# 23 more products of constants on TensorE in the head of a quantized Hadamard FFN

## What is computed

```python
def reference(x, itok, L0_cond_weights, w_up, w_down):
    w = L0_cond_weights[itok]                        # (64, 64, 64)
    h = einsum('bct,bcd->bdt', x, w)                 # projection
    h = hbitlinear(h, w_up, 8)                       # 512 -> 1024
    h = jnp.square(jax.nn.relu(h))
    return x + hbitlinear(h, w_down, 8)              # 1024 -> 512

def hbitlinear(x, w, bits):
    xq = act_quant(fwht(x), bits)      # Hadamard along the last axis, absmax rounding per token
    wq = weight_quant(w)               # round(w / mean|w|), clipped to -1..1, times mean|w|
    return einsum('bsd,fd->bsf', xq, wq)
```

## Time and profile before

| | us |
|---|---|
| median of 3 timed runs | 263.11 |
| lowest and highest of them | 262.69, 263.40 |
| the profiled execution | 261.73 |
| its span, first to last instruction | 259.7 |
| TensorE busy | 247.4 (95%) |
| VectorE busy | 207.1 (80%) |
| ScalarE busy | 147.5 (57%) |
| GpSimd busy | 107.9 (42%) |

### The profile page before, as it was taken

How to read it: one execution, slowest core, us unless ns; L and a number is a source line. 1 busy time by engine, 2 the same in 40 slices (tenths; PEclk the granted TensorE clock), 3 DMA queues, 4 the chain that set the end, 5 groups by cost and what they waited for, 6 DMA issues and landing times. The chain is left out here.

```text
span 259.7 us, 6271 instructions
## 1 busy us (share of the span) xinstructions
PE 247.4 (95%) x2172; PEld 205.7 (79%) x2172; DVE 207.1 (80%) x344; ACT 147.5 (57%) x210; POOL 107.9 (42%) x135
## 2 busy tenths in 40 slices
PE   8589999998999999999999999999999999989994
PEld 8478898987898788878897787978898887757651
DVE  0548679988788697989878986989898888999482
ACT  0378887676554775475656365565775646651330
POOL 1000006661624508080806444372936445786710
PEclk9959999999999999999999999999999999999999
DMA  3995061475268444675564881464535657424523
GB/s 106 361 373 180 16 213 32 59 180 98 52 161 130 87 163 82 122 174 118 141 91 121 189 198 36 79 203 85 130 71 126 167 139 107 121 79 121 128 105 138
DMA packets 63441, 34.29 MB, mean 132 GB/s; under 512 B 53554, under 2 KB 53682, under 8 KB 63410
## 3 DMA queue, kind: packets, MB, share of 16 engines
q10 hardware_dynamic: 48370, 12.95, 28.3%
q1 hardware_dynamic: 15040, 20.95, 25.3%
HBM read 13.70 MB, written 8.39 MB: 85 GB/s over the span
## 5 line engine op out<-in xcount | busy, mean ns | idle before, releaser
L373 POOL TENSOR_TENSOR p<-g 128x512 f32<-128x512 f32 x64 | 80.8, 1286 | 128.1 <-DVE g L1237 128.1
L907 PE MATMUL h_ps<-zqT,w_upT 128*128 128x256 f16 x512 | 63.5, 273 | 0.7 <-DMA zqT<-zq 0.7
L930 PE MATMUL u_ps<-had_sb,p 128*128 128x128 f32 x480 | 58.8, 276 | 1.2 <-ACT uq L566 1.2
L930 PEld LDWEIGHTS u_ps<-had_sb,p 128*128 128x128 f32 x480 | 56.7, 192 | 3.5 <-ACT uq L566 1.7
L962 PE MATMUL o_ps<-w_downT,uqT 128*128 128x512 f16 x240 | 56.7, 379 | 0.2 <-DVE uqT L1211 0.2
L907 PEld LDWEIGHTS h_ps<-zqT,w_upT 128*128 128x128 f16 x512 | 49.3, 98 | 8.7 <-issue 0.9
L526 ACT ACTIVATE g<-h_ps 128x512 f32<-128x512 f32 x64 | 37.3, 595 | 26.9 <-PE h_ps L907 19.3
L566 ACT ACTIVATE uq<-u_ps,u_mul 128x1024 f16<-128x1024 f32 x30 | 33.4, 1113 | 33.0 <-DVE u_mul L1255 29.1
L1244 DVE TENSOR_REDUCE u_max<-u_ps 128x1 f32<-128x1024 f32 x30 | 36.6, 1220 | 11.3 <-PE u_ps L930 10.9
L962 PEld LDWEIGHTS o_ps<-w_downT,uqT 128*128 128x128 f16 x240 | 23.4, 98 | 22.3 <-issue 0.4
L1232 DVE TENSOR_TENSOR g<-g 128x1024 f32<-128x1024 f32 x32 | 40.8, 1300 | 0.1
(11 more groups left out here) (52 smaller groups left out, 126.4 us busy)
## 6 DMA issues: line engine op xcount, KB each, us to landing
xs<-in_x_dram SPq DMA_DIRECT2D x16, 512.0 KB, 3.8
out_dram<-out_sb SPq DMA_DIRECT2D x32, 256.0 KB, 2.3
w_raw<-in_L_ffn_w_down_dram SPq DMA_DIRECT2D x4, 512.0 KB, 5.9
w_raw<-in_L_ffn_w_up_dram ACTq DMA_DIRECT2D x2, 512.0 KB, 6.0
w_raw<-in_L_ffn_w_up_dram SPq DMA_DIRECT2D x2, 512.0 KB, 6.8
ws<-in_L_cond_weights_dram SPq DMA_DIRECT2D x62, 16.0 KB, 2.6
uqT<-uq ACTq DMA_TRANSPOSE x30, 3.5
zqT<-zq ACTq DMA_TRANSPOSE x15, 4.0
```

What stands on the lines that cost most here:

```text
L373: nc.gpsimd.tensor_tensor(new[:, :, m, :], old[:, :, 0, :], old[:, :, 1, :], (ALU.add, ALU.subtract)[m]).then_inc(s_p8[k], 1)
L907: mm = nc.tensor.matmul(h_ps[:, u % 2, i, :].rearrange("p (k n) -> p k n", k=KP), w_upT[:, q, f * P:(f + 1) * P], zqT[t % NZT][:, :, q, :] ...
L930: mm = nc.tensor.matmul(home[:, c * P:(c + 1) * P], p8[t % 2][:, c, k * P:(k + 1) * P], had_sb[:, :], start=True, stop=True)
```

## The change

The loop of `warm` becomes a helper, `idle(n, home)`, which issues n products of `ones` with itself into a given place. `warm` has 17 of them instead of 16, now into the first 128 columns of h_ps. 4 more stand before project(0), 10 before had_z(0, 1), 6 before weight_sum(0) and 2 before first_turn(0); these write columns 256 to 383 of o_ps, which nobody reads before `down` writes them. That makes 39 products instead of 16. The helper has no wait of its own and signals nothing. The lists of ScalarE, VectorE, GpSimd and SyncE are as they were.

```diff
-WARM = 16
+WARM = 17
...
             def warm():
                 pe.wait_ge(s_const, 1)
-                for i in range(WARM):
-                    nc.tensor.matmul(o_ps[:, 0:P], ones[:, :], ones[:, :], start=True, stop=True)
+                idle(WARM, h_flat[:, 0:P])
+
+            def idle(n, home):
+
+                for i in range(n):
+                    nc.tensor.matmul(home, ones[:, :], ones[:, :], start=True, stop=True)
...
             warm()
+            idle(4, o_ps[:, 2 * P:3 * P])
             project(0)
+            idle(10, o_ps[:, 2 * P:3 * P])
             had_z(0, 1)
+            idle(6, o_ps[:, 2 * P:3 * P])
             weight_sum(0)
             had_z(0, 0)
             project(1)
             weight_turn(0, 1)
             weight_turn(0, 0)
+            idle(2, o_ps[:, 2 * P:3 * P])
             first_turn(0)
             first_turn(1)
             had_z(1, 0)
```

## The result

The changed kernel takes 259.8 us in the median (259.37 to 260.16), the kernel before 262.9 us (262.45 to 263.40) beside it. The ratio is 0.9881, with a 95% interval from 0.9855 to 0.9907: 3.1 us faster, 1.2%. The prediction said 261.4 us and a range from 260.2 to 263.2.

What follows compares the result with a forecast made beforehand. TensorE was taken to bound the kernel after the head. Savings of 0.2, 0.92 and 0.59 us sum to 1.7; the 1.73 us inherited through VectorE, off 263.11, gives 261.4 us, range 260.2 to 263.2.

Steps and rivals of the forecast that it cites:

- The bound: TensorE has nothing left to give after the head, so a microsecond won in the head should reach the end.
- The price of a product, and the four places: 0.22 us each at full clock, 0.44 at half; at most 0.1 us late before project(0), had_z(0,1), weight_sum(0) and first turn.
- The clock: In the head, filling TensorE's waits removes the 6.82 us stretch at 0.50 (12.40 to 19.22); granted clock stays 1.00.
- The sum for the profiled execution: weight_sum(0) 0.2, had_z(0,0) 0.92, project(1) 0.59 us; VectorE's y_outer(1,1) passes on 1.73 us, up(0,1) at 22.43, span 258.0.
- From the profile to the time: Whole kernel: the profiled execution's 1.73 us is taken off the timed median of 263.11 us, giving 261.4 us.
- The rival with the larger gain: Low clock rises later in timed runs, slowing all of project(1) and the transposes; 2.9 us won, 260.2 us; 12%.
- The slower rivals: Two cases, at weight_sum(0) and at the turns, in which the clock falls all the same; 264.5 and 264.8 us; together 9%.
- The one at weight_sum(0): Clock falls at 12.4 anyway and the six products delay weight_sum(0) by up to 1.4 us; 264.5 us; 5%.
- The one at the turns: Clock falls among the transposes behind project(1), near 22 us; up to 3.4 us lost against 1.73 won, 264.8 us; 4%.
- Given back: Behind the head, turned z or u, a transfer or fixed orders keep 0 to 0.8 us; 262.3 to 263.1 us; 16%.

Runs made afterwards that it cites:

- the sixth: Head of the kernel before with only the five more products ahead of project(0); 262.47 us, ratio 0.9995 to the kernel before.
- the moved loads: Kernel before with the loads of x 4 and 5 issued early, behind that of x 3; 263.29 us, ratio 1.0012.
- a late head at full clock: Changed kernel with eighteen products ahead of weight_sum(0) in place of six; 262.19 us in the median.
- twelve: Changed kernel with twelve products ahead of weight_sum(0) in place of six; 260.51 us.

## Why the prediction was wrong

*The bound.* Right. TensorE is the bound behind the head, and what the head wins reaches the end, less 0.36 us in the profile.

*The price of a product, and the four places.* Right at full clock. The five ended later than 8.1 (project(0) at 8.51), because the first constants were longer at half clock: seventeen took 6.69 us, where the sixteen took 6.00 us in the earlier trace rows and 5.34 to 6.53 us in the other profiles of the kernel before. (This low stretch is read from the durations; the granted clock stands at 1.00 in the view from its start on, so the earlier trace rows does not show the rise at 5.57 that the prediction names.) Neither this nor had_z(0,1) at 12.83 instead of 12.3 cost anything, because weight_sum(0) waits for ScalarE until 15.45. The wait left there was 0.22 instead of 0.9 us, and 0.84 us in the second profile.

*The clock.* Right: without the pauses it stays at 1.00. That the five and the two do nothing was their stated price of nothing; the experiment with the ten and the six bears it out.

*The sum for the profiled execution.* Right to 0.05 us: up(0,1) was to start at 22.43 and did at 22.48. The span was to be 258.0 and is 258.4 us. The path behind the 0.05 us was in part another: weight_abs(1,0) started at 18.15, 0.2 us before its forecast, but y_split(1) at 18.97 instead of 18.84, and y_outer(1,1) waited 0.25 us for it. Two small misses cancelled.

*From the profile to the time.* This is the step that failed: "I take the same step off". The 1.7 us hold for an execution in which the stretch at 0.50 ends at 19.22, in the middle of project(1). In the four other heads it ends at 20.33 to 21.55. The term that was mis-sized is project(1), put at 0.59 us: it gives back 1.04, 1.50, 1.67 and 1.68 us there (3.10, 3.56, 3.73 and 3.74 minus 2.06 us). The head's gain is then 2.3 to 2.8 us, 2.7 us in the middle one of the five (2.5 us with the sixth).

*The rival with the larger gain.* Its mechanism was this one, and its 2.9 us and 260.2 us are the nearest to the measured 3.1 and 259.8 us. How near is in part luck: it put 0.6 us more on project(1), which gives back up to 1.09 us more than the forecast's 0.59, and as much again on the transposes, which took 1.07 us in all six heads, so that nothing came back there. It got 12% where the profile gave a reason for more: all timed runs lay 0.96 to 1.67 us above the profiled one, and none of the later profiles of this head has the clock back before 19.22. The range ended at that rival's middle value, with nothing beyond it for the waits behind the head.

*What is left.* 3.1 minus 2.7 us is 0.4 us, 0.6 us by the six heads. The candidates are the longer low stretches of the few executions at a mean clock of 0.98, and waits of up(1,0) for the turned zqT near 35 to 40 us. Such a wait of 1.2 to 1.9 us stands in four of the seventeen profiles: two of five of the kernel before (counting the moved loads), one of three with a late head at full clock, and the one with transposes; in none of four of the changed kernel, the ten and six, and twelve. These four are the only ones in which the turning of z of tile 1 took 5.1 to 5.8 us from issue to landing; in the other thirteen it took 3.2 to 3.6 us. So the wait goes with a slow landing. What makes the landing slow is not shown, nor is it that a late head meets it more often: the counts are small, the version with transposes has it with an early head, and moving the loads that I suspected did not help. By the medians, a late head at full clock costs 0.8 us more than it is late.

*The slower rivals.* The one at weight_sum(0) was seen without the ten, at 0.56 us of delay instead of 1.4, outweighed by the earlier return of the clock. The one at the turns did not occur. *Given back* occurred with 0.36 us in the profile, within the noise of such waits.

## What to carry to other kernels

A profile shows one position of the clock's low stretch against the work; before pricing its removal, slide the stretch over the neighbouring work and look at where the timed runs lie against the profiled one. If they lie above it, the profile may be of a lucky execution and the gain larger than it says. Fill pauses with work nobody waits for, in the place where a wait covers it, and no more of it than the wait: six products too many cost 0.8 us.

## What the runs showed of the hardware

- The clock fell from 2.4 to 1.2 GHz inside pauses of TensorE of 2.2 to 2.5 us, or up to 1.0 us after the end of pauses of 2.0 to 2.8 us, with TensorE at work again (behind the 2.8 us at 63.02: at 63.98). Such a pause did not always bring it down: with one of 2.3 us left (the ten alone), five of twelve executions had a mean clock of 0.998 to 1.0. With the pauses at 1.16 and 0.91 us it stayed up in each of six.
- The start and the end of the low stretch differ between executions of the same program by over 2 us (it ended from 19.22 to 21.55), at nearly the same mean clock. The mean clock alone does not tell how much it cost.
- The low stretch lasted 6.83 us in all five profiles of the old head, with a pause of TensorE inside it, and 3.41 us in the two in which TensorE worked on without a pause (the six in place, and behind 63.02).
- Transposes of a constant held the clock as well as fp32 products did.
- From issue to landing the turning of z of tile 1 took 3.2 to 3.6 us in thirteen profiles and 5.1 to 5.8 us in four, and TensorE waited 1.2 to 1.9 us for it in just those four.
